# A transformer block and a second attention on one core: keys and values of the second attention projected in the feed-forward's first half, in three passes, with the second attention spread over two sequences

## The reference, cut to what matters

```python
h1 = _ln(x, ln1_g, ln1_b)
x = _attn(h1, h1, a1_wq, a1_wk, a1_wv, a1_wo, a1_bo, d_q1, d_k1, d_v1, d_w1) + x
h2 = _ln(x, ln2_g, ln2_b)
x = _attn(h2, context, a2_wq, a2_wk, a2_wv, a2_wo, a2_bo, d_q2, d_k2, d_v2, d_w2) + x
h3 = _ln(x, ln3_g, ln3_b)
hg = h3 @ ff_w1 + ff_b1                  # 512 -> 2 * 2048
a, g = jnp.split(hg, 2, axis=-1)
x = a * jax.nn.gelu(g, approximate=False) @ ff_w2 + ff_b2 + x
...
h = layernorm(hidden_states, ln1_w, ln1_b)   # hidden_states is x
x = layernorm(inputs, ln2_w, ln2_b)          # inputs is ctx_1024
q = (h @ Wq.T + bq)...
k = (x @ Wk.T + bk)...
v = (x @ Wv.T + bv)...
scores = jnp.einsum('bhqd,bhkd->bhqk', q, k) / jnp.sqrt(jnp.float32(dqk))
probs = jax.nn.softmax(scores, axis=-1)
return hidden_states + jnp.einsum('bhqk,bhkd->bhqd', probs, v)...
```

## Time and profile before

| | us |
|---|---|
| median of 3 runs | 3019.38 (3018.3 to 3019.39) |
| the profiled execution, its own time | 3019.96 |
| its span, first to last instruction | 3018.2 |
| PE busy in it | 2806.9 (93%) |
| DVE, ACT, POOL busy | 1771.2, 1455.2, 692.1 |
| DMA queue of all transfers, share of 16 engines | 22.0% |

### The profile page before, as it was taken

One profiled execution on the slowest core, in us unless ns is written; L12 is line 12 of the kernel. 1 busy time (PEld: TensorE's weight loads), 2 busy tenths in 40 slices (PEclk: granted clock), 3 DMA queues, 4 the chain that ended last, 5 costly groups with the idle time before them and its releaser, 6 DMA issues. The chain is left out here.

```text
span 3018.2 us, 54146 instructions
## 1 busy us (share of the span) xinstructions
PE 2806.9 (93%) x17920; PEld 2214.6 (73%) x17920; DVE 1771.2 (59%) x4484; ACT 1455.2 (48%) x3763; POOL 692.1 (23%) x1147
## 2 busy tenths in 40 slices
PE   5799999999999996699999997999999999999997
PEld 5566666666666663599999996888888888888885
DVE  6799899999999986433333335344444444444432
ACT  4577777777777765211111112444444444444442
POOL 1222222222222221133333322112111111111110
PEclk8899999999999997799999998999999999999997
DMA  4443343333333342400010004000000000000000
GB/s 144 83 82 80 80 85 85 79 84 85 83 80 80 87 77 54 152 29 28 28 42 28 28 21 140 22 28 35 28 28 28 28 28 28 28 28 28 35 15 14
DMA packets 325753, 169.11 MB, mean 56 GB/s; under 512 B 274240, under 2 KB 290624, under 8 KB 325696
## 3 DMA queue, kind: packets, MB, share of 16 engines
q1 hardware_dynamic: 325696, 168.39, 22.0%
HBM read 76.07 MB, written 25.17 MB: 34 GB/s over the span
## 5 line engine op out<-in xcount | busy, mean ns | idle before, releaser
L595 ACT ACTIVATE e<-S,bias,qk_scale 128x256 f32<-128x256 f32 x1024 | 563.6, 564 | 65.3 <-DVE e L707 61.4
L690 DVE TENSOR_REDUCE negmax<-S 128x4 f32<-128x1024 f32 x256 | 312.0, 1219 | 105.3 <-PE S L503 103.7
L707 DVE TENSOR_SCALAR e<-e,rsum 128x256 f16<-128x256 f32 x1024 | 291.8, 348 | 2.5
L565 ACT ACTIVATE shifted<-PJ,round_col,inv 128x512 f32<-128x512 f32 x192 | 149.4, 778 | 227.5 <-PE PJ L157 226.5
L1584 POOL TENSOR_TENSOR mid_partsB<-mid_actB,mid_partsB 128x256 fp32r<-128x256 f32 x128 | 102.1, 797 | 611.8 <-DVE mid_partsB L1482 611.8
L148 PE MATMUL PJ<-w_a_wo,oT 128*128 128x512 f32 x512 | 239.6, 612 | 2.6 <-ACT oT L604 1.8
L157 PE MATMUL PJ<-hT,w_a_wq 128*128 128x256 f32 x1536 | 208.3, 294 | 21.5 <-DVE hT L685 17.7
L157 PEld LDWEIGHTS PJ<-hT,w_a_wq 128*128 128x128 f32 x1536 | 195.4, 199 | 35.5 <-issue 35.5
L595 ACT ACTIVATION_READ_ACCUMULATOR e<-S,bias,qk_scale 128x1 f32 x1024 | 209.1, 204 | 0.0
L157 PE MATMUL AG0A<-h_partsA,upA 128*128 128x256 f32 x1536 | 200.0, 287 | 7.2 <-POOL h_partsA L1579 3.4
L157 PE MATMUL AG0B<-h_partsB,upB 128*128 128x256 f32 x1536 | 199.1, 286 | 7.6 <-POOL h_partsB L1579 6.4
(11 more groups left out here) (186 smaller groups left out, 5578.8 us busy)
## 6 DMA issues: line engine op xcount, KB each, us to landing
x_in<-in_x_dram SPq DMA_DIRECT2D x16, 512.0 KB, 3.5
ctx_in<-in_ctx_dram SPq DMA_DIRECT2D x16, 512.0 KB, 3.5
mid_dram<-x SPq DMA_DIRECT2D x16, 512.0 KB, 2.7
y_inA<-mid_dram SPq DMA_DIRECT2D x16, 512.0 KB, 3.6
part_dram<-x3A SPq DMA_DIRECT2D x16, 512.0 KB, 4.0
y_inB<-mid_dram SPq DMA_DIRECT2D x16, 512.0 KB, 3.2
kv_in<-in_ctx_dram SPq DMA_DIRECT2D x16, 512.0 KB, 4.7
baseB<-part_dram SPq DMA_DIRECT2D x16, 512.0 KB, 3.2
```

Of the source, the lines that this page charges most:

```text
L565: nc.scalar.activation(shifted[:, bank, :], PJ[bank][:], ACT.Identity, bias=round_col[:, 0:1], scale=inv[:, d:d + 1]).then_inc(pj_emptied[ ...
L595: nc.scalar.activation(e[:, s, i, :], S[s][:, i // 2, i % 2, :], ACT.Exp, bias=bias[:, s, i:i + 1], scale=qk_scale[:, ph.a:ph.a + 1], accu ...
L690: nc.vector.tensor_reduce(negmax[:, g % 2, :], S[g % 2][:].rearrange("p i q n -> p (i q) n"), AX_X, ALU.max, negate=True).then_inc(max_don ...
L707: nc.vector.tensor_scalar(e16[:, s, i, :], e[:, s, i, :], rsum[:, s, i:i + 1], ROUND16, ALU.mult, ALU.add).then_inc(prob_scaled, 1)
```

## The change

It touches both halves and nothing ahead of them.

1. `Wk` and `Wv` are now loaded and split in pass 0 of half A and `Wq` in pass 0 of half B, each in two pieces of 512 KB (`act_w2_high`, `dve_w2_low`). k, v and q are made with split products (line 157): 24 of 256 columns or 12 of 512 to a bank. Their other operand is split too, on ACT, DVE and POOL, into `parts4`.
2. Half A normalises and turns the context (before up 4 of a pass), projects k and v behind and between its last down products, and stores them to `k_dram` and `v_dram`. It also stores `h3T` to `h3_dram`.
3. Half B loads `h3T`, k and v in place of x and the context, and has no turn of `h3T` or `cT`, no k and no v.
4. In half B, the turn of the last norm and q of sequence b - 1 stand in pass b (into banks Y, behind up 1). Pairs 0, 1 and part of 2 of sequence b - 1 are done in pass b, the rest and the turn back of sequence b - 2 at its start. The drain behind the last pass holds the rest of sequence 14 and all of sequence 15.

The core of the diff (the engines' other sequences follow the same order; `act_k`, `act_v`, `dve_k`, `dve_v`, `act_q` and `dve_q` empty the banks as before, into `k_out`, `v_out` and `q4`):

```diff
-            w2 = {n: sb(both_halves, "w_" + n, [P, KC, D]) for n in ("Wq", "Wk", "Wv")}
+                W2 = ("Wq",) if attends else ("Wk", "Wv")
+                w2 = {n: sb(two, "w_" + n, [P, 2, KC, D], F32R) for n in W2}
...
                     if name == "v":
-                        ins = by_token(AG[j], w2["Wv"], cT, j)
+                        ins = by_token_split(AG[j], w2["Wv"], parts4, j)
                     else:
-                        ins = by_channel(AG[j], w2["W" + name], h4T if name == "q" else cT, j)
+                        ins = by_channel_split(AG[j], w2["W" + name], parts4, j)
...
+                def pe_sequence_a(pe, b, last=False):
+                    pe.wait_ge(h3_low_done, 2 * (b + 1))
+                    for f in range(HC):
+                        if f == CT_TURN_AT:
+                            for j in range(2):
+                                pe_turn(pe, b, "cT", j)
+                        if f == H3_TURN_AT and not last:
+                            for j in range(2):
+                                pe_turn(pe, b, "h3T'", j)
+                        pe_up(pe, b, f)
+                        if f >= 2:
+                            pe_down(pe, b, f - 2)
+                    pe_project(pe, b, "k", 0)
+                    pe_down(pe, b, HC - 2)
+                    pe_project(pe, b, "k", 1)
+                    pe_down(pe, b, HC - 1)
+                    for j in range(2):
+                        pe_project(pe, b, "v", j)
...
+                def dve_parts4(dve, n):
+                    nc.vector.tensor_copy(parts4[:, 0, 2:4, :], turned4T[:, 2:4, :]).then_inc(high4_done[1], 1)
+                    dve.wait_ge(high4_done[1], n)
+                    nc.vector.tensor_tensor(parts4[:, 1, 2:4, :], turned4T[:, 2:4, :], parts4[:, 0, 2:4, :],
+                                            ALU.subtract).then_inc(low4_done, 1)
...
+                    if new:
+                        dve_max4(dve, b - 1, 2)
+                    dve_x3(dve, b)
+                    dve.wait_ge(x3_done, TT * (b + 1))
+                    ln_stats(dve, ln4, x3, b)
+                    ln_xhat(dve, ln4, x3, xhat2, b)
...
+                        def moves_b(b, s, old, done, heads, pairs, res_n):
+                            sp.wait_ge(x3_done, done)
+                            load_base(b)
+                            load_k(s, heads)
+                            load_v(s, pairs)
+                            store_out(old, res_n)
```

More of the change, by code:

```diff
@@ L1199, in pe_project, with pe_turn_h4 @@
+                def pe_turn_h4(pe, s, j):
+                    pe.wait_ge(ln4["xhat_done"], TT * (s + 1))
+                    transpose_chunks(Y[j], xhat2, j).then_inc(h4_filled[j], 1)
+                def pe_project(pe, b, name, j):
                     pe.wait_ge(ag_emptied[j], fill2(b, name))
-                    for i in range(2):
-                        pe.wait_ge(xt_emptied[i], ln_no(b, "h4T" if name == "q" else "cT", last) + 1)
+                    pe.wait_ge(low4_done, 2 * b if name == "q" else 2 * (b + 1))
+                    if first(b) or (attends and isinstance(b, int)):
+                        pe.wait_ge(w2_low_done, 2 * len(W2))
@@ L1323, in affine_of @@
[L1323 to L1326, removed]
-                    return dst(), g, cols[base_name + "_b"]
+                    pe_project(pe, b, "k", 1)
+                    pe_down(pe, b, HC - 1)
+                    for j in range(2):
+                        pe_project(pe, b, "v", j)
@@ new lines, in act_exp4 @@
+                def act_exp4(act, s, p):
+                    for h in (2 * p, 2 * p + 1):
+                        act.wait_ge(max4_done, H1 * s + h + 1)
+                        if h == 0 and not first(s):
+                            act.wait_ge(rsum4_done, s)
+                        for qt in range(TT):
+                            nc.scalar.activation(e4[:, h % 2, qt, :], X4[h % 2][:, qt, :], ACT.Exp,
+                                                 bias=negmax4[:, h % 2, qt:qt + 1],
+                                                 accum_out=sums4[:, qt, h:h + 1]).then_inc(exp4_done, 1)
@@ L1405, in act_sequence2 @@
[L1405 to L1421 removed]
+                        if f == CT_TURN_AT:
+                            act_post_c(act, b)
@@ new lines, in pool_sequence_a, with pool_sequence_b @@
+                        if f == 3 and not last:
+                            ln_rstd(pool, ln4, turn_no(b, "h3T'"))
+                        if f == CT_TURN_AT:
+                            pool_low4(pool, b + 1)
+                    if not last:
+                        pool_h3_low(pool, b + 1)
+                def pool_sequence_b(pool, b, new=True, last=False):
+                    for f in range(HC):
+                        pool_mid_low(pool, b, f)
+                        if new and f == 1:
+                            pool_low4(pool, b)
+                        if new and f == 6:
+                            pool_x3_bv(pool, b - 1)
+                    if not last:
+                        pool_h3_low(pool, b + 1)
+                    ln_rstd(pool, ln4, b)
@@ L1681, in _, with store_h3 @@
-                        if attends:
-                            loads(B - 2, B - 1, B, None)
-                        for b in range(B - 3, B):
-                            store(b, TT * (b + 1))
-                        sp.wait_ge(stored, 16 * B + 1)
+                        def store_h3(b, turns):
+                            for j in range(2):
+                                sp.wait_ge(xt_emptied[j], turns)
+                            sp.dma_start(h3_mid[b], h3T[:]).then_inc(h3_stored, 16)
```

935 lines of the change are left out of this document (591 added, 344 removed).

## The result

The changed kernel took 2921.54 us (median of 4 runs, 2920.33 to 2923.19) beside 3018.84 us for the kernel before (4 runs, 3018.18 to 3019.39). The ratio is 0.9675, with a 95% interval of 0.9661 to 0.969, so 3.25% or 97 us less. The profiled execution took 2920.33 us with a span of 2918.5 us; against the span of 3018.2 before, that is 99.7 us less.

The account below looks back on a forecast made before the run. PE's queue was taken to bound both halves; the changes per pass, border and drain summed to -79.7 us, taking the span from 3018.2 to 2938.5 and the forecast to 2938 us, range 2920 to 2960 (0.82).

Parts of the forecast that it names:

- drain: Behind half B's last pass: 58.3 us for 65.1, so -6.8, with the first scores of sequence 15 at about 23.5.
- half A, pass 0: First pass of half A, with the new weights' loads between the chunks: 60.9 us for 47.0, so +13.9.
- half A, passes 1 to 15: Steady passes of half A with a turn, k and v added on PE: 47.5 us each, +178.5 in all.
- border: From the end of half A's last product to up 0 of half B: 12.8 us for 20.6, so -7.8.
- half B, pass 0: First pass of half B, without k, v, q and turns but with some late ups: 42.1 us for 60.0, -17.9.
- half B, passes 2 to 14: Steady passes of half B with k, v, turns and a wait removed: 54.6 us for 71.8, -223.6 in all.
- half B, pass 15: Last pass of half B, to its last down product: 54.6 us for 47.9 before, so +6.7.
- the prediction's rival: Three passes don't pay: split v, k and q still take 3.45 a bank, 58 us come back, 2996; chance 0.04.
- the norm chain: Norm of x in half B's passes: xhat there at 5.3 us, wanted by PE at 6.6, holding by 1.3.
- v's load: In half B, SP may load v some 12.3 us before its first use; a load takes up to 4.7.
- joints that it rounded against itself: Joints in half B, with v at 2.8 and A's pauses: three places rounded up that could give 8 us more.
- The rival of a wait that opens in half B: Norm chain 0.6 to 2 us late, up to 28 us: 2946 to 2966; 0.15, shared with a longer pass 0.

Follow-up runs that it names:

- the last two experiments: Changed kernel with the old drain order and chunk 3 loaded first, 1735.73 us; kernel before with the new drain order, 1821.71 us; both without the first stage.
- the fourth experiment: Changed kernel with six more additions of 512 columns on DVE ahead of the statistics of half B's last norm: 2979.38 us, ratio 0.9863.

## Why the prediction was right, and where it was off

The forecast was 2938 us in 2920 to 2960, and the time is 2921.54: faster, as said, but 1.5 us above the lower end of the range. The saving of 80 us was forecast a fifth too small. That the time is still inside is luck in part: the reasons given for 2920 (all margins hold, a faster v, no more in pass 0) do not include the drain, which alone saved 9.6 us more than forecast. The sum by its own terms, in us, each measured from the rows in the same way as it was worked out:

| term | predicted | measured | from |
|---|---|---|---|
| start of half A | 0 | -1.9 | up 0 at 1237.59 for 1239.48 |
| half A, pass 0 | +13.9 | +15.2 | 62.2 us |
| half A, passes 1 to 15 | +178.5 | +177.0 | 47.43 us a pass |
| border | -7.8 | -6.1 | 2010.0 to 2024.48 |
| half B, pass 0 | -17.9 | -21.1 | 2024.48 to 2063.35 |
| half B, pass 1 | -22.7 | -23.4 | 48.36 us |
| half B, passes 2 to 14 | -223.6 | -229.3 | 13 x (54.14 - 71.78) |
| half B, pass 15 | +6.7 | +6.3 | 54.2 us for 47.9 |
| drain | -6.8 | -16.4 | 48.7 us for 65.1 |
| sum | -79.7 | -99.7 | span: -99.7 |

**Right, and shown by runs.** That half B's passes go by PE's queue: 0.87 us added to it came back as 0.88 in a pass, and PE is busy for 54.14 of 54.14 us. In half A the longer banks of plain float32 came back in full as well. That three split products take 2.87 us for a bank's 3.45: putting plain float32 back cost 58.4 us, where the prediction's rival had priced it at 58. That the norm chain is ready 5.3 us into the pass and holds by 1.3: ready at 5.35, with 1.28 to spare, and 1.2 us put into it cost nothing in the passes.

**Right, by the trace alone.** That v's load has ample room: 11.4 us for a transfer of 3.3. No run made it longer.

**Off: the drain, half of the miss (9.6 of 20 us).** Two steps of the prediction failed there. It let q and its turns run at the low clock and put the first scores of sequence 15 at 23.5 us behind the last down product; they stand at 19.5, since only the four turns behind the wait of 5.08 us run slowly (1.06 us where 0.60 is usual) and q takes 3.15 us. And it took from the old drain's 41.5 us only the product with v and its waits, 6.7 us in three places; it left the rest at its old, low clock. But the low clock went for the most part with the old order, as the last two experiments show from both sides: the order took 3.8 to 4.4 us of waits and 5.2 to 6.5 us of slow products with it. From the first scores to the end the new drain takes 2918.5 - 2889.34 = 29.2 us, where the prediction had 34.8. The rows 5.64 and 9.07 of the earlier trace rows were there to be read that way: the step without a product with v was short, and the matmuls in the long one (0.79 for 0.48 us) were slow.

**Off by a little: half B's passes, 54.6 for 54.14 (5.7 us in all).** The prediction had named this as joints that it rounded against itself. The pieces below half a microsecond were not taken apart further. Pass 0 of half B was overpriced by 3.2 us: up 2 waited 1.15 us and up 4 0.62, where the count of transfers in the queue had given 3.4 and 2, and only up 0 ran at the low clock. Half A has a small wait that the prediction did not list: DVE normalises x only behind the split of the turned context (from 1322.79 to 1323.79), and the turn of x waits 0.19 us for it in each pass, 2.9 us over 15 passes. The faster v hid that in the sum.

**Off the other way: the places where one queue of SP feeds the weights.** Pass 0 of half A lasted 62.2 for 60.9, and the border 14.5 for 12.8, since h3T was issued only at 2014.08 and the first chunk reached ACT at 2020.19. For pass 0 of half A the cause is shown in the main: what stood ahead of chunk 3 in the queue. For the border it is read from the trace alone.

**v.** Taken at 2.8 us a bank from the nearest row of the first stage, measured 2.72, which is 2.6 us over 16 passes. The rule of the Trainium skill that the prediction had weighed (FP8 and Floating Point Precision, TensorE Precision Notes: true FP32 takes four passes) would have three of them at 0.75 of the time, an estimate from that page. Measured are 2.87 / 3.45 = 0.83 with 256 columns and 2.72 / 3.44 = 0.79 with 512, so here the rows were the better guide.

The rival of a wait that opens in half B did not come, but the fourth experiment shows that its price was set too low: a late end of 2.3 us cost 3.95 in each pass.

## What to carry to other kernels

When the bounding engine has no idle time, work out its queue item by item; such a sum held within 1% for every steady pass here, and a margin beside it could be used up nearly to its end at no cost in those passes. In stretches where that engine waits again and again, do not carry over durations from the old rows: the order of the work decides the waits, and here more than half of what a better order gave came from products that ran at a higher clock, not from the waits themselves. Put the next independent product into the place where PE would wait for a softmax, also in a drain of 40 us: that alone was worth 10 us in each of two kernels.

## What the hardware showed that I had not expected

- After only 2.2 to 2.4 us without a product, in a kernel that had been busy at full clock, the granted clock fell to 0.58 and the next 24 products took 4.60 us instead of 3.12. Waits of 0.25 to 0.82 us, many in a row, left it at 1.0 in the changed kernel's drain: window 2880 to 2910, in which PE was busy for 23.2 of 30 us. But the same waits did not in the kernel with plain float32, where it fell in one of the steps.
- Waits of 1.83 and 1.2 us in turn, as the old order of the drain has them, went with a mean of 0.58 over the 20.1 us that followed, though PE was busy for 13.3 of them; only the scores that open the fourth step ran at full clock (0.48 us).
- The split product gained more in the form with 512 columns: 0.79 of the time of plain float32, for 0.83 with 256.
